# Softmax in the score banks: the differences, the exponentials and their sums move from SBUF to PSUM

## The reference

```python
HEADS, DIM_HEAD, WINDOW = 16, 64, 32
def local_attention(q, k, v):            # q, k, v: [8, 16, 512, 64]
    bk2, bv2 = look(bk), look(bv)        # own window of 32 keys and the one before: 64 keys
    sim = jnp.einsum('bhwie,bhwje->bhwij', bq, bk2) * QK_SCALE
    sim = jnp.where(mask, -jnp.finfo(sim.dtype).max, sim)
    attn = jax.nn.softmax(sim, -1)
    return jnp.einsum('bhwij,bhwje->bhwie', attn, bv2)
...
for i in range(6):
    x = attn_layer(shift_tokens(x), Wqkv[i], q_scale[i], k_scale[i], Wo[i]) + x
    x = ffn_layer(shift_tokens(x), ln_g[i], ln_b[i], W1[i], b1[i], W2[i], b2[i]) + x
```

## Time and profile before

| | |
|---|---|
| median of 3 runs | 3763.29 us (3762.48 to 3780.51) |
| the profiled execution | 3773.0 us, its span 3771.0 us, 2.0 us lie around the span |
| TensorE busy | 3375.2 us, 90% of the span |
| VectorE busy | 3287.8 us, 87% |
| GpSimd busy | 2810.7 us, 75% |
| ScalarE busy | 2435.9 us, 65% |
| mean granted TensorE clock | 0.962 of full speed |

### The profile page before, as it was taken

The page is one execution under the profiler, slowest core; times in us unless marked ns, Lnnn a source line. Parts: engine busy times, 40 slices in busy tenths (PEclk is TensorE's granted clock), DMA queues, the critical chain, the costliest instruction groups (busy, mean ns, idle before and its releaser), DMA issues.

```text
span 3771.0 us, 107872 instructions
## 1 busy us (share of the span) xinstructions
PE 3375.2 (90%) x45916; PEld 2204.0 (58%) x46108; DVE 3287.8 (87%) x2914; ACT 2435.9 (65%) x3945; POOL 2810.7 (75%) x1265
## 2 busy tenths in 40 slices
PE   5758999998999999999998999899999999999987
PEld 3325665665665665665666666565666656666664
DVE  6758999998999988999898998898988988998992
ACT  4645766766766766666666676666666666666764
POOL 4457788778787778778777778877777887887771
PEclk9879999999999999999999999999999999999996
DMA  2001111121111111111111111121111111111111
GB/s 72 1 1 36 36 34 38 34 58 41 35 34 39 34 51 44 39 34 35 36 52 44 33 35 35 31 50 44 39 33 34 38 46 45 39 37 35 34 37 36
DMA packets 129694, 141.98 MB, mean 38 GB/s; under 512 B 35388, under 2 KB 73152, under 8 KB 129216
## 3 DMA queue, kind: packets, MB, share of 16 engines
q1 hardware_dynamic: 129216, 135.09, 14.5%
HBM read 19.62 MB, written 2.10 MB: 6 GB/s over the span
## 4 chain that ended last, share of the span: by engine, by line
PE 33%; DVE 23%; POOL 18%; issue 12%; ACT 4%; SPq 3%; DMA 2%; POOLq 0%; ACTq 0%; DVEq 0%
PE bank L570 10%; POOL rr L1138 8%; POOL swp L1148 5%; PE mid L620 4%; DVE Pr L1362 4%; DVE rot L1398 4%; PE mid L579 4%; DVE raw L1390 4%; PE bank L639 4%; PE bank L668 3%; DVE rot L1404 3%; PE mid L607 2%; PE mid L627 2%; DVE ss L1384 2%; PE bank L676 2%
## 5 line engine op out<-in xcount | busy, mean ns | idle before, releaser
L1148 POOL TENSOR_TENSOR swp<-raw,TS 128x1024 f32<-128x1024 f32 x384 | 899.6, 2370 | 622.0 <-DVE raw L1390 622.0
L570 PE MATMUL bank<-wqkv,xs 128*128 128x512 f32 x2304 | 1206.9, 627 | 24.1 <-DMA xs<-F 8.6
L1138 POOL TENSOR_TENSOR rr<-ssm,nhalf 128x32 f32<-128x32 f32 x192 | 1214.8, 6327 | 16.0
L896 ACT ACTIVATE raw<-bank 128x512 f32<-128x512 f32 x768 | 434.6, 592 | 545.0 <-DVE rot L1404 483.8
L579 PEld LDWEIGHTS mid<-ident,rot 128*128 128x128 f32 x3072 | 367.8, 143 | 387.7 <-issue 335.9
L579 PE MATMUL mid<-ident,rot 128*128 128x128 f32 x3072 | 444.6, 278 | 132.7 <-DVE rot L1404 127.3
L1384 DVE TENSOR_REDUCE ss<-sq 128x16 f32<-128x1024 f32 x384 | 463.6, 1207 | 112.1 <-ACT sq L904 111.3
L570 PEld LDWEIGHTS bank<-wqkv,xs 128*128 128x128 f32 x2304 | 387.3, 193 | 289.9 <-issue 194.0
L1390 DVE TENSOR_TENSOR raw<-raw,rr 128x2048 f32<-128x2048 f32 x192 | 469.3, 2444 | 42.6 <-POOL rr L1138 42.6
L1398 DVE TENSOR_TENSOR rot<-raw,TC 128x2048 f32<-128x2048 f32 x192 | 442.2, 2303 | 52.6 <-PE mid L579 51.1
L1404 DVE TENSOR_TENSOR rot<-rot,swp 128x2048 f32<-128x2048 f32 x192 | 440.2, 2292 | 21.0 <-DVE rot L1398 1.4
(11 more groups left out here) (132 smaller groups left out, 4340.8 us busy)
## 6 DMA issues: line engine op xcount, KB each, us to landing
PT<-PTd SPq DMA_DIRECT2D x1344, 64.0 KB
xs<-F SPq DMA_DIRECT2D x192, 64.0 KB, 1.9
BT<-PTd SPq DMA_DIRECT2D x192, 64.0 KB
wqkv<-d_wqkv SPq DMA_DIRECT2D x36, 256.0 KB, 2.8
fwo<-d_fwo SPq DMA_DIRECT2D x6, 512.0 KB, 4.3
d_out<-X SPq DMA_DIRECT2D x8, 256.0 KB, 2.3
w<-d_w SPq DMA_DIRECT2D x6, 341.0 KB
w<-d_w SPq DMA_DIRECT2D x6, 128.0 KB
```

The lines of the kernel that those rows point to most:

```text
L570: nc.tensor.matmul(bank[bk][:, :], xs[:, j, :], wqkv[:, c, :], start=True, stop=True)\
L1138: pool.tensor_tensor(rr[:, :], ssm[:, :], nhalf[:, :], ALU.pow).then_inc(rr_ready, 1)
L1148: last = pool.tensor_tensor(dst[:, :, :, t, :], src[:, :, :, 1 - t, :], tab.unsqueeze(2).broadcast_to([P, 2, HEADS, 32]), ALU.mult)
```

## The change

VectorE's `less_max` writes its differences back over the scores in PSUM, ScalarE's `exps` works there in place, and `sums` and `probs` read PSUM. `probs` is now the step that moves the values to `Pr` in SBUF. No instruction is added or removed, none changes its place in any engine's list, and the shapes stay. TensorE's `scores` of a tile waits for `probs` of the tile before, where it waited for `less_max`. A second edit lies in ScalarE: the first of the four `to_raw` copies of tile n waits until the sine and cosine products of tile n - 2 have read `raw`, where it waited until their sum was made. Four hunks like the first differ only in place and stand here once.

```diff
@@ TensorE, in each of the four kinds of slot @@
-                    after(c, (4, sub_ready))
+                    after(c, (4, prob_ready))
                     step(c, 3, scores)
@@ -892,7 +892,8 @@
             def to_raw(n, b, j, c, first):
                 act.wait_ge(proj_done[c], n + 1)
                 if first:
-                    wait(act, rot_ready, n - 1)
+                    wait(act, sin_ready, n - 1)
+                    wait(act, cos_ready, n - 1)
@@ -934,7 +935,7 @@
             def exps(n, b, j):
                 act.wait_ge(sub_ready, n + 1)
-                nc.scalar.activation(Pr[:, :], Pr[:, :], ACT.Exp).then_inc(exp_ready, 1)
+                nc.scalar.activation(mid[:, 1:3, :], mid[:, 1:3, :], ACT.Exp).then_inc(exp_ready, 1)
@@ -1342,14 +1343,13 @@
             def less_max(n, b, j):
                 dve.wait_ge(max_ready, n + 1)
-                nc.vector.tensor_tensor(Pr[:, :].rearrange("p (u k) -> p u k", k=DH),
-                                        mid[:, 1:3, :].rearrange("p h (u k) -> p (h u) k", u=HH),
-                                        mx[:, :].unsqueeze(2).broadcast_to([P, HEADS, DH]), ALU.subtract)\
+                sc = mid[:, 1:3, :].rearrange("p h (u k) -> p (h u) k", u=HH)
+                nc.vector.tensor_tensor(sc, sc, mx[:, :].unsqueeze(2).broadcast_to([P, HEADS, DH]), ALU.subtract)\
                     .then_inc(sub_ready, 1)
             def sums(n, b, j):
                 dve.wait_ge(exp_ready, n + 1)
-                nc.vector.tensor_reduce(sm[:, :], Pr[:, :].rearrange("p (u k) -> p u k", k=DH), AX.X, ALU.add)\
+                nc.vector.tensor_reduce(sm[:, :], mid[:, 1:3, :].rearrange("p h (u k) -> p (h u) k", u=HH), AX.X, ALU.add)\
                     .then_inc(sum_ready, 1)
@@ -1359,7 +1359,8 @@
             def probs(n, b, j):
                 pr = Pr[:, :].rearrange("p (u k) -> p u k", k=DH)
                 dve.wait_ge(rsum_ready, n + 1)
-                nc.vector.tensor_tensor(pr, pr, rs[:, :].unsqueeze(2).broadcast_to([P, HEADS, DH]), ALU.mult)\
+                ex = mid[:, 1:3, :].rearrange("p h (u k) -> p (h u) k", u=HH)
+                nc.vector.tensor_tensor(pr, ex, rs[:, :].unsqueeze(2).broadcast_to([P, HEADS, DH]), ALU.mult)\
                     .then_inc(prob_ready, 1)
```

## The result

| | median | range | ratio to before, 95% interval |
|---|---|---|---|
| before, run beside it (4 runs) | 3766.91 us | 3762.48 to 3780.51 | |
| changed kernel (4 runs) | 3858.94 us | 3848.43 to 3864.86 | 1.0235 [1.0198, 1.0272] |

The change makes the kernel 2.35% slower, by 92 us. The forecast was slower, at 3885 us; it was 26 us too high. The span of the profiled execution is 3861.1 us, the mean granted TensorE clock 0.949 against 0.962.

The account below looks back on a forecast made before the run. The prediction took the TensorE-VectorE hand-over through `rot`, with its clamp-against-cosine-product order, as the bound. It summed 3773 + 155 - 14 - 20 = 3894, less 10 us for the profiled run: 3885 us; 8 in 10 range 3675 to 3955.

Parts of the forecast that it names:

- What the shorter `probs` triggers: In slots with c % 4 == 3 the cosine product starts ahead of GpSimd's clamp `ssm`; loss of 155 us.
- late batches: Batches where `ssm` starts after the cosine product and is held off; 16 before, all 47 intervals forecast, about 5 us each.
- Probs: VectorE's product at L1362, with one PSUM input, no longer waits for GpSimd: 1225 ns, 116 us of work back.
- the rival by which nothing changes: `probs` with one PSUM input still waits for GpSimd, so the time stays 3763 us; chance 0.10.
- the 100 us that the forecast had named as a sign: Sign of being right: VectorE's busy time falls by over 100 us while the span grows.
- copies and bands: TensorE waits less for ScalarE's earlier copies, 14 us, and for the DMAs of PT, 20 us; 34 us gained.
- nothing of the gain by earlier L1398 is left in such a batch: In a late slot an earlier cosine product gains nothing, as it has to wait for `FX` to end.
- The bound of 57.7 us: Upper bound for the earlier copies: TensorE's whole wait for them; a quarter, 14 us, was taken.
- Sums, less_max, exps and the new wait of scores: PSUM operands add 22 ns a tile on VectorE, hidden; TensorE's wait for the previous tile's `probs` costs 0.
- A second late `ssm`: Rival: in slots with c % 4 == 2 the clamp also comes late, 60 us more, 3945 us; chance 0.17.
- The gain arrives: Rival: clamp order stays, shorter `probs` pays, 3671 us, or 3590 us if the clamp always comes first; chance 0.23.

Follow-up runs that it names:

- e3: Changed kernel plus a wait: in slots with c % 4 == 3 VectorE's cosine product waits until GpSimd's clamp of the next tile is done; 3650.12 us.
- e5: Changed kernel with GpSimd's `norms` split in slots with c % 4 == 3: clamp ahead of `FX`, power behind it; 3612.1 us.
- e6: Kernel before, with GpSimd's clamp in slots with c % 4 == 3 also waiting for VectorE's block transpose; 3897.17 us.
- e7: Changed kernel with the sums of every fourth tile made twice, the second time into a tile nobody reads; 3713.44 us.
- e11: e5 with the exponentials written to SBUF and `probs` and sums reading SBUF; differences stay in the bank, copies early; 3685.66 us.
- e4: Kernel before with the same added wait as e3, cosine product held for the clamp in slots with c % 4 == 3; 3712.15 us.
- e1: Kernel before with only the earlier copies: first copy waits for the sine and cosine products instead of their sum; 3767.0 us, ratio 0.9973.
- e2: Changed kernel without the earlier copies: they wait for the sum again, softmax stays in the banks; 3869.49 us.
- e12: e5 without the earlier copies: the first copy of a tile waits for the sum as before; 3610.91 us.
- e10: Kernel before with `norms` split as in e5, clamp ahead of `FX`; 3694.04 us, ratio 0.9786.
- e9: e5 plus, in all slots, the cosine product held until the clamp of the next tile is done; 3603.24 us, ratio 0.9548.

## Why the prediction was right, point by point

**What the shorter `probs` triggers.** This was the deciding term, and mechanism and place held. `ssm` starts 0.55 or 0.74 us behind the transposes in most batches, as forecast, and late batches went from 16 to 45 (forecast 47). e3 and e5 (order put right, loss gone), e6 (order spoilt in before, loss there) and e7 (more work, less time) show it as the cause. The margin was thinner than forecast: in the late batches of after the cosine product is ahead of `ssm` by 0.05 to 0.64 us, in half of them by 0.28 us or less, where 0.45 was worked out. That hardly a batch fell on the other side has some luck in it.

**The size of that term** was too high, and with it the forecast. Taking each of the 47 intervals between the starts of `FX` by itself, the 16 late ones of before average 74.45 us (73.1 to 76.0) and the 31 others 70.40 us, so a late batch costs 4.1 us. The forecast had 75.2 us for a late one, where the earlier trace rows give 75.5 for one single interval, among the longest of the 16; from this came its 5.0 us. 29 more late batches at 4.06 us cost 118 us, where 155 stood. The mean interval went from 71.8 to (3814.7 - 348.2) / 47 = 73.8 us, and 47 x 1.97 = 93 us is the whole loss.

One sentence was too coarse, that the order of the two starts decides by itself. It decides through `rr`: only when VectorE reaches `normed` before `rr` ends does `normed` catch `vpe`. The batch at 1972 us has a late `ssm`, e5 and the earlier trace rows have a caught `rr`, and none of them loses anything.

**Probs.** Forecast 1225 ns, measured 1206 to 1224, which also rules out the rival by which nothing changes. The Trainium skill, "GPSIMD Engine Reference", section 1, names contention for VectorE instructions with two SBUF inputs; the runs agree, and e11 against e5 puts the price of keeping the exponentials in SBUF at 74 us here. The 116 us of work that it was to save left 92.5 us on VectorE as a whole, below the 100 us that the forecast had named as a sign: the cosine product took 10.0 us more in all, `normed` 4.7 us.

**What is gained beside it.** 118 - 93 = 25 us were gained in the rest, where 34 stood for copies and bands. The late batches of after average 73.94 us against 74.45, 0.5 us shorter. So the forecast took 155 - 118 = 37 us too much loss and 34 - 25 = 9 us too much gain, and that makes up the 26 us that it missed to within 2 us. The sentence that nothing of the gain by earlier L1398 is left in such a batch was roughly right: where no batch is late the change gains more, 70.46 - 69.16 = 1.3 us a batch between e4 and e3.

**The bands and the copies.** TensorE's wait for PT fell from 40.6 to 24.4 us, 16 where 20 were taken. The copies gave about 10 us where 14 were taken (e1, e2), and nothing once the late batches were gone (e12). The bound of 57.7 us was the wrong sort of number: that wait moved to other releasers.

**Sums, less_max, exps and the new wait of scores.** `less_max` takes 1232 ns into PSUM against 1225 into SBUF, `sums` 1214 ns against 1209: 12 ns a tile where 22 were taken. By the Trainium skill, "VectorE: DVE Perf Modes", section on the TRN2 errata, both PSUM readers would be 65 ns longer, an estimate from its fixed parts; the runs don't show it, and the measurement decides. No wait of `scores` for `probs` is among the waits of after.

**The rivals.** A second late `ssm`, in the slots with c % 4 == 2, did not come: only two of the 48 cases there are over 2 us. The clamp starts 0.10 us ahead of the transposes' end in most of those slots and the cosine product 0.11 us behind it; that is a margin of 0.2 us, which the forecast had taken for none. "The gain arrives" is what the change is worth without the race: 3650 us in e3 and 3612 us in e5, between that rival's 3671 and its 3590.

**The account from the race-free side.** With the split, before gains 3767 - 3694 = 73 us (e10) and the changed kernel 3859 - 3612 = 247 us (e5); with the wait it is 3767 - 3712 = 55 us (e4, taken from the same 3767) and 209 us (e3). So the race takes 174 or 154 us more from the changed kernel than from before, and without it the change gains 82 or 62 us; the difference is the 92 us of loss both times. This is the same runs added up another way and no further proof. Nor is all that the split gains the price of late batches: the intervals of e5 average 68.4 us, those of e3, where none is late either, 69.2.

What stays open: the 25 us gained in the rest are about the 16 us of the bands and the 10 of the copies, but each of these is small beside the spread of the runs, so the agreement can be chance; why 10 batches of e7 are late; and whether e9 is really faster than e5.

## What to carry to other kernels

Where a small instruction of one engine and a long one of another start within a few tenths of a microsecond of each other and can hold each other off, the order of the two is part of the kernel's design: pin it with a wait or move the small one ahead before anything upstream is tuned, or a gain upstream will flip it. Read the margins of such starts from the timeline first, since a table of busy times can't show them, and follow the late one through to where someone waits: here it took three catches in a row before TensorE stood still. With the clamp moved ahead, the same change that lost 2.35% is part of a kernel that beats before by 4% to 4.5% (e5, e9).

## What the runs showed of the hardware

A small GpSimd instruction that starts while VectorE is in a product of two SBUF inputs lasts until that product is over: 2.33 us for the 128x4 addition `vpe` that takes 0.23 us alone, 2.33 for 0.29 us at the 128x32 clamp; and `rr` takes 7.48 us for 5.46. The other way round `rr` holds VectorE off little: at 1972 us L1405 starts 0.24 us behind `rr` and takes its usual 2.29 us. With one input in PSUM the VectorE product doesn't wait for GpSimd (1206 to 1224 ns), and where the long products are kept behind the clamp, as in e9, the clamp beside it is never over 338 ns.

A stall of TensorE has a second price, that had not been counted apart. Windows of after around the end of the stall at L658, at 1099.73; after the window's length come busy times of PE, PEld, DVE, ACT and POOL, then the granted clock, the DMA share and GB/s:

```profile
1097.00:1098.00 1.00, 0.00 (x0) 0.00 (x0) 1.00 (x2) 0.00 (x0) 0.92 (x2) 1.00 0.00 0
...
1099.70:1101.00 1.30, 1.27 (x5) 1.25 (x6) 0.04 (x1) 1.30 (x3) 1.30 (x2) 0.50 0.00 0
...
1104.00:1105.00 1.00, 1.00 (x7) 1.00 (x6) 1.00 (x1) 1.00 (x3) 1.00 (x1) 0.51 0.03 9
1105.00:1106.00 1.00, 1.00 (x10) 1.00 (x10) 0.17 (x1) 0.66 (x2) 1.00 (x1) 1.00 0.00 0
```

The clock falls to 0.50, the level of 1.2 GHz, during the stall, and is back at 1.00 after 1105. In these 5.3 us TensorE works slower: four products of L658 take 1.09 us where they take 0.63 in e3. From the start of L658 at 1099.73 to the first product of L570 behind the sixteen of L639, at 1105.82, it is 6.09 us; the same stretch in e5, from 1111.14 to 1114.68 with the clock at 1.00, is 3.54 us. So about 2.6 us are lost beside the 4.63 of waiting. Not all of that is on the path, since a late batch costs 4.1 us. The mean granted clock of the kernels goes down with the late batches, 0.949 with 45, 0.962 with 16 and 0.979 in e5 with none, though not by them alone: e4 has none and stands at 0.969.
